# A gated-state attention block between two feed-forwards: each head's state update as a 64-column matmul of its own, and a state read that alternates the heads

## The chip, the cores and the metric
One core of a Trainium2 chip runs the whole program in one launch. The metric is the device time in microseconds; the median of several runs is compared. TensorE's clock has two levels, 1.2 and 2.4 GHz; the profile gives the granted clock as a share of the full one.

## The reference
The input x has 2 sequences of 1024 tokens, 512 wide. The program computes x + 0.5 FFN(norm(x)), then adds attention of the normed result, then adds 0.5 FFN(norm(x)) again. The feed-forward is a two-expert layer with top-1 routing. The change is in the attention alone. It has 16 heads, keys of 64, values of 128 and 64 memory slots per head. With s the clipped slot logits, z their running logsumexp, p = exp(s - z) and g = exp(z[t-1] - z[t]), it is two scans over time:

```python
def step_k(hk, x):
    q_t, k_t, p_t, g_t = x
    hk = hk * g_t[:, :, None, :] + k_t[..., None] * p_t[:, :, None, :]
    return (hk, jnp.einsum('bhk,bhkm->bhm', q_t, hk))
pvT = jax.nn.softmax(okT, axis=-1)
def step_v(hv, x):
    pv_t, v_t, p_t, g_t = x
    hv = hv * g_t[..., None] + p_t[..., None] * v_t[:, :, None, :]
    return (hv, jnp.einsum('bhm,bhmv->bhv', pv_t, hv))
```

The result of the second scan is normed per head, multiplied by a gate and projected by Wo. hk (64 x 64 per head) is called the key state below, hv (64 x 128 per head) the value state.

## The kernel before
The attention works on pairs of heads: eight pairs, the first seven in a hardware loop on every engine, the last written out once more. Within a pair there are four units k = 0 to 3 of 512 tokens, two per sequence, and in a unit four chunks cc of 128 tokens. The scans are done chunk by chunk without the running maximum: with e = exp(s), the state before a chunk is the sum over the earlier chunks of e^T k (key state) or e^T v (value state), and within a chunk a masked score matrix gives the rest. z is the running sum of e, and its reciprocal rz scales the result. A unit with k even starts a sequence ("first" in the code): its chunk 0 has no state to read, so 3 chunks read one, and it forms 4 updates, the last for the next unit. A unit with k odd reads a state in 4 chunks and forms 3 updates.

On 128 partitions the tiles hold both heads of the pair: head h in the partitions 64h to 64h + 63 for what is laid out by feature (qT, kT, eT, pT), and in the columns 64h to 64h + 63 for what is laid out by token (en, kn, the transposed e and k). PSUM is used as six banks R[0] to R[5] of 128 x 512 fp32 and two banks PJ for projections. Plain fp32 tiles go through TensorE as fp32; the projections are split by hand into high and low fp32r parts, three matmuls per product.

The order of TensorE's work in a unit is written out by hand, with the projections of the next unit put between the steps of this one: transposes of z (L1208), project_q of the next unit (L1128), the key state update (L1219, into R[5], signals dk_mm), the scores k^T q of each chunk and head (L1225, heads alternating, 64 partitions each), project_k, the read of the first scan (L1237 with hk, L1239 with the masked scores am; signals ok_mm), project_s and project_vg 0 (L1128, L1154), transposes of the scaled ok (L1250), project_vg 1, the scores of the second scan (L1258, heads alternating, 64 partitions each), the value state update (L1266, signals dv_mm), the masked scores times v (L1273, R[0] and R[1] by head, waits for b_masked), the read of the value state (L1278, waits for hv_done, signals o_mm after each head), project_vg 2 and 3 (L1154), transposes of u (L1294, waits for u_done), transposes of e and k for the next unit (L1191, L1195), and the output projection (L1307).

L1219 multiplies all 128 columns of kn by all of en for a chunk, so the result also has the two products of one head with the other, which nothing reads. L1266 multiplies all 128 columns of en by both heads' 256 columns of v; its four chunks fill two banks, R[2] and R[3], with a signal per bank, and hv is 256 wide, of which each head uses its own half.

VectorE adds the updates up: hk in L1019 and L1021 (64 x 64 pieces, one per head), hv in L1065 and L1067 (one 128 x 256 piece per chunk), each waiting for the one before. Before hv it masks the second scan's scores (L1056), after it come gate_make (L940) and the running sum z_scan (L932). Then follows the chain to the output: ScalarE squares R[0] and R[1] (L887) as the two o_mm signals arrive, VectorE sums (L1085) and adds (L1088), GpSimd raises to the power -0.5 (L772), VectorE multiplies into u (L1092), and TensorE transposes u (L1294).

Before the first pair a ring of six buffers of 512 columns, taken from am, u and hv, receives the rows gathered by DMA from the first feed-forward. In the last pair VectorE, ScalarE and GpSimd also do the norm and routing for the second feed-forward, and there is no next unit after the last one.

Of the kernel before, what the change touches and what calls it, by code (L numbers as in the profile page):

```python
# [28 lines left out]
P = 128  # L29
# [24 lines left out]
UC = UNIT // CHUNK  # L54
# [574 lines left out]
def phase_attention(nc, top, c, watt, gnorm, slot_rows, gather_row, half_weight, xres, norms, routing, loaded, sorted_rows, aw):  # L629
# [9 lines left out]
    with ExitStack() as ctx:  # L639
# [18 lines left out]
        hv = sb("at_hv", [P, UC, 2 * DV])  # L658
# [15 lines left out]
        ring = [x[:, n * D // width:(n + 1) * D // width, :].rearrange("p a b -> p (a b)") for x, width in  # L674
                ((am[:, :, :, :].rearrange("p a b c -> p (a b) c"), P), (u[:, :, :, :].rearrange("p a b c -> p (a b) c"), DV), (hv, 2 * DV)) for n in range(2)]
# [229 lines left out]
        def _(dve):  # L905
# [99 lines left out]
            def pair(i, last_pair):  # L1005
                for k in range(UNITS):
# [47 lines left out]
                    for b in range(2):  # L1054
                        dve.wait_ge(b_mm, count(i, k, 2, b))
                        dve.tensor_tensor(am[:, b, :, :],  # L1056
                                          R[4 + b][:, :].rearrange("p (a t) -> p a t", a=4),
                                          c["causal"][:, :].rearrange("p (a t) -> p a t", a=1).to_broadcast([P, 4, P]), ALU.mult).then_inc(b_masked, 1)
                    for cc in range(UC if first else UC - 1):
                        to = (cc + 1) % UC  # L1060
                        if cc % 2 == 0:
                            dve.wait_ge(dv_mm, count(i, k, 2, cc // 2))
                        part = R[2 + cc // 2][:, (cc % 2) * 2 * DV:(cc % 2 + 1) * 2 * DV]
# [54 lines left out]
        def _(pe):  # L1118
# [80 lines left out]
            def pair(i, last_pair):  # L1199
                for k in range(UNITS):  # L1200
# [17 lines left out]
                    for cc in range(UC if first else UC - 1):  # L1218
                        last = pe.matmul(R[5][:, chunk(cc)], kn[:, cc, :], en[:, cc, :], start=True, stop=True)  # L1219
# [43 lines left out]
                    for b in range(2):  # L1263
                        for a in range(2 if first or b == 0 else 1):
                            cc = 2 * b + a
                            last = pe.matmul(R[2 + b][:, a * 2 * DV:(a + 1) * 2 * DV], en[:, cc, :], v[:, b2, cc, :], start=True, stop=True)  # L1266
                        last.then_inc(dv_mm, 1)
# [8 lines left out]
                    for h in range(2):  # L1276
                        for cc in range(1 if first else 0, UC):
                            last = pe.matmul(R[h][:, chunk(cc)], pT[half(h), chunk(cc)], hv[half(h), cc, h * DV:(h + 1) * DV],  # L1278
                                             start=False, stop=True, skip_group_check=True)
                        last.then_inc(o_mm, 1)  # L1280
# [102 lines left out]
```

## Time and profile before

| | |
|---|---|
| runs, median (lowest to highest) | 2237.46 us (2235.6 to 2238.39), 3 runs |
| profiled execution, span from first to last instruction | 2232.7 us |
| median run beside that span | 4.8 us more |
| TensorE busy with matmuls | 2074.2 us, 93% of the span |
| VectorE busy | 1417.0 us, 63% |
| ScalarE busy | 688.9 us, 31% |
| GpSimd busy | 282.5 us, 13% |
| granted TensorE clock, mean | 0.979 |

The profiled execution's time is known as its span; what lies around it is taken from the difference to the median. A row of the trace gives an engine's instruction or a run of equal ones: start, duration, engine, line, operation, output and inputs, shape, count, and where the engine was idle before it, for how long and what released it. Matmuls are pipelined, so the duration of one is longer than its share of the stream: the distance between the starts of two stages tells what the first one costs. "PE ... 64*128" is a matmul on 64 rows and 128 columns of the array.

### The profile page before, as it was taken

What the parts mean: (1) busy time and instruction counts of PE and PEld (TensorE: products, weight loads), DVE (VectorE), ACT (ScalarE), POOL (GpSimd) and SP (SyncE); (2) the same over time, 40 slices, a digit from 0 to 9 for tenths busy, and PEclk for the clock granted to TensorE, in tenths of its full rate; (3) what the DMA queues carried; (4) which work ended last, traced back from release to release, by engine and by line L of the source; (5) the groups of instructions that cost most, each with busy time, mean ns of one, the idle gap of its engine ahead of it and who ended that gap; (6) DMA issues with size and microseconds to landing.
All of it is one profiled execution on the core that took longest, in us unless ns stands there. A gap on an engine that the chain in (4) does not pass through costs nothing. (4 is left out here: it accounts for less than half of the span.)

```text
span 2232.7 us, 29878 instructions
## 1 busy us (share of the span) xinstructions
PE 2074.2 (93%) x11280; PEld 1739.2 (78%) x11280; DVE 1417.0 (63%) x2579; ACT 688.9 (31%) x1188; POOL 282.5 (13%) x243
## 2 busy tenths in 40 slices
PE   0999999969999999999999999999999569999996
PEld 0888888858888888888888888878888458888885
DVE  6665666766666665665666666665668655665666
ACT  2443444533121221212222221222223134443443
POOL 4000001031020110110110110200202230000004
PEclk9999999979999999999999999999999779999998
DMA  5332333430010000000100100100100062433336
GB/s 205 134 132 94 132 119 130 154 102 8 1 36 9 8 29 8 17 27 1 33 11 1 36 8 1 36 8 1 36 1 20 38 161 95 133 130 101 119 119 245
DMA packets 46926, 149.50 MB, mean 67 GB/s; under 512 B 5856, under 2 KB 5856, under 8 KB 46816
## 3 DMA queue, kind: packets, MB, share of 16 engines
q1 hardware_dynamic: 38544, 121.13, 16.8%
q0 software_dynamic: 8272, 26.76, 3.6%
q8 instruction: 87, 1.43, 0.3%
q14 instruction: 23, 0.19, 0.0%
HBM read 125.83 MB, written 22.04 MB: 66 GB/s over the span
## 5 line engine op out<-in xcount | busy, mean ns | idle before, releaser
L1154 PE MATMUL at_pj<-at_w_lo,at_xT_hi 128*128 128x512 f32 x512 | 207.1, 405 | 0.0
L1154 PE MATMUL at_pj<-at_w_hi,at_xT_hi 128*128 128x512 f32 x512 | 201.0, 392 | 0.0
L1154 PE MATMUL at_pj<-at_w_hi,at_xT_lo 128*128 128x512 f32 x512 | 200.6, 392 | 0.0
L1128 PE MATMUL at_pj<-at_xT_hi,at_w_lo 128*128 128x512 f32 x384 | 162.0, 422 | 0.8 <-DVE at_xT_lo L969 0.8
L503 DVE TENSOR_TENSOR first_ff_w_lo<-first_ff_stage,first_ff_w_hi 128x1024 fp32r<-128x1024 f32 x80 | 98.0, 1225 | 101.1 <-ACT first_ff_w_hi L365 101.1
L503 DVE TENSOR_TENSOR last_ff_w_lo<-last_ff_stage,last_ff_w_hi 128x1024 fp32r<-128x1024 f32 x80 | 97.9, 1224 | 99.4 <-ACT last_ff_w_hi L365 99.4
L1128 PE MATMUL at_pj<-at_xT_lo,at_w_hi 128*128 128x512 f32 x384 | 153.0, 398 | 0.0
L1128 PE MATMUL at_pj<-at_xT_hi,at_w_hi 128*128 128x512 f32 x384 | 152.8, 398 | 0.0
L772 POOL TENSOR_TENSOR at_coef<-at_ms,minus_half 128x4 f32<-128x4 f32 x64 | 63.6, 1010 | 590.9 <-DVE at_ms L1088 590.9
L748 POOL TENSOR_TENSOR at_w_lo<-at_stage,at_w_hi 128x1024 fp32r<-128x1024 f32 (+1 forms) x36 | 78.4, 2178 | 416.7 <-ACT at_w_hi L812 416.7
L1108 DVE TENSOR_TENSOR xres<-at_r,xres 128x512 f32<-128x512 f32 x128 | 88.1, 688 | 61.2 <-PE at_r L1307 61.2
L365 ACT ACTIVATE last_ff_w_hi<-last_ff_stage 128x1024 fp32r<-128x1024 f32 x80 | 84.8, 1060 | 128.2 <-PE last_ff_ps_y L609 117.9
L365 ACT ACTIVATE first_ff_w_hi<-first_ff_stage 128x1024 fp32r<-128x1024 f32 x80 | 84.8, 1060 | 126.4 <-PE first_ff_ps_y L609 118.0
L597 PE MATMUL last_ff_ps_h<-last_ff_xT_hi,last_ff_w_lo 128*128 128x512 f32 (+1 forms) x320 | 119.1, 372 | 3.4 <-DVE last_ff_w_lo L503 2.4
L597 PE MATMUL first_ff_ps_h<-first_ff_xT_hi,first_ff_w_lo 128*128 128x512 f32 (+1 forms) x320 | 118.2, 369 | 1.5 <-DVE first_ff_factor L535 1.3
L597 PE MATMUL first_ff_ps_h<-first_ff_xT_lo,first_ff_w_hi 128*128 128x512 f32 (+1 forms) x320 | 117.8, 368 | 0.0
L597 PE MATMUL last_ff_ps_h<-last_ff_xT_hi,last_ff_w_hi 128*128 128x512 f32 (+1 forms) x320 | 117.7, 368 | 0.0
L597 PE MATMUL first_ff_ps_h<-first_ff_xT_hi,first_ff_w_hi 128*128 128x512 f32 (+1 forms) x320 | 117.7, 368 | 0.0
L597 PE MATMUL last_ff_ps_h<-last_ff_xT_lo,last_ff_w_hi 128*128 128x512 f32 (+1 forms) x320 | 117.7, 368 | 0.0
L1010 DVE RECIPROCAL at_rz<-at_r 128x512 f32<-128x512 f32 x32 | 107.2, 3349 | 11.3 <-PE at_r L1208 11.3
L1154 PEld LDWEIGHTS at_pj<-at_w_lo,at_xT_hi 128*128 128x128 f32 x512 | 96.2, 188 | 22.7
L609 PE MATMUL last_ff_ps_y<-last_ff_w_hi,last_ff_a_lo 128*128 128x512 f32 x288 | 113.1, 393 | 0.8 <-DVE last_ff_a_lo L547 0.8
(283 smaller groups left out, 4921.8 us busy)
## 6 DMA issues: line engine op xcount, KB each, us to landing
first_ff_stage<-wff SPq DMA_DIRECT2D x80, 512.0 KB, 3.2
last_ff_stage<-wff SPq DMA_DIRECT2D x80, 512.0 KB, 3.3
at_stage<-watt SPq DMA_DIRECT2D x24, 512.0 KB, 3.7
at_stage<-watt SPq DMA_DIRECT2D x16, 384.0 KB, 3.3
xres<-x SPq DMA_DIRECT2D x4, 1024.0 KB, 10.2
first_ff_xg<-sorted_rows SPq DMA_DIRECT2D x4, 1024.0 KB, 6.4
slot_rows<-first_ff_y POOLq DMA_DIRECT2D x4, 1024.0 KB, 5.4
last_ff_xg<-sorted_rows SPq DMA_DIRECT2D x4, 1024.0 KB, 7.3
```

What stands on the lines that cost most here:

```text
L365: act.activation(w_hi[:, t % RING, :], stage[:, t % RING, :], ACT.Copy).then_inc(w_hi_done, 1)
L503: dve.tensor_tensor(w_lo[:, t % RING, :], stage[:, t % RING, :], w_hi[:, t % RING, :].bitcast(F32), ALU.subtract).then_inc(w_lo_done, 1)
L597: last = pe.matmul(ps_h[t % 2][:, 0:width], w[:, r, k * P:(k + 1) * P], x[:, k, 0:width], start=(k == 0 and n == 0), stop=(k == KC - 1 and ...
L609: last = pe.matmul(ps_y[i][:, :], x[:, r, i * P:(i + 1) * P], w[:, r, D:2 * D], start=(t == 0 and n == 0), stop=(t == HT - 1 and n == 2))
L748: pool.tensor_tensor(w_lo[:, col:col + width], stage[:, 0:width], w_hi[:, col:col + width].bitcast(F32), ALU.subtract).then_inc(piece_lo, 1)
L772: pool.tensor_tensor(coef[:, cols], ms[:, cols], c["minus_half"][:, cols], ALU.pow).then_inc(coef_done, 1)
L1010: dve.reciprocal(rz[:, :, :], R[2][:, :].rearrange("p (a b) -> p a b", a=UC)).then_inc(rz_done, 1)
L1108: dve.tensor_tensor(xres[:, k * UC + cc, :], R[4 + cc % 2][:, :], xres[:, k * UC + cc, :], ALU.add).then_inc(added, 1)
L1128: last = pe.matmul(PJ[(7 * k + part) % 2][:, :], wq(w, kk, part), x[:, kk, tok], start=(kk == 0 and n == 0), stop=(kk == KC - 1 and n == 2))
L1154: last = pe.matmul(PJ[(7 * k + 3 + t) % 2][:, :], x[:, kk, tok], wvg(w, kk), start=(kk == 0 and n == 0), stop=(kk == KC - 1 and n == 2))
```

## The change
For each chunk the key state update becomes two matmuls, one per head: 64 columns of kn as the stationary operand, 64 columns of en moving, and the result in the head's own half of the partitions. The value state update becomes two matmuls as well: 64 columns of en stationary, the head's 128 columns of v moving, the result in its half of the partitions of R[2], one bank for all four chunks and a single signal dv_mm. hv is 128 wide, and VectorE's additions with it. The read of the value state loops over chunks outside and heads inside, so o_mm is signalled by the last two matmuls. The gather ring takes rz in place of the second half of hv.

```diff
--- before.py
+++ after.py
@@ -655,7 +655,7 @@
         rz = sb("at_rz", [P, UC, P])
         am = sb("at_am", [P, 2, UC, P])
         hk = sb("at_hk", [P, UC, P])
-        hv = sb("at_hv", [P, UC, 2 * DV])
+        hv = sb("at_hv", [P, UC, DV])
         ok = sb("at_ok", [P, UC, P])
         pv = sb("at_pv", [P, UC, P])
         pT = sb("at_pT", [P, UNIT])
@@ -671,8 +671,8 @@
         R = [ctx.enter_context(nc.psum_tensor(f"at_r{b}", [P, 512], F32)) for b in range(6)]
 
 
-        ring = [x[:, n * D // width:(n + 1) * D // width, :].rearrange("p a b -> p (a b)") for x, width in
-                ((am[:, :, :, :].rearrange("p a b c -> p (a b) c"), P), (u[:, :, :, :].rearrange("p a b c -> p (a b) c"), DV), (hv, 2 * DV)) for n in range(2)]
+        ring = [x[:, n, :, :].rearrange("p a b -> p (a b)") for x in (am, u) for n in range(2)]
+        ring += [x[:, :, :].rearrange("p a b -> p (a b)") for x in (hv, rz)]
         xn = [x[:, :, :].rearrange("p a b -> p (a b)") for x in (en, kn, ok, pv)]
         row_added, shift_done, xn_done, x_turned = sem("at_row_added"), sem("at_shift_done"), sem("at_xn_done"), sem("at_x_turned")
         x_hi, x_lo = sem("at_x_hi"), sem("at_x_lo")
@@ -1056,11 +1056,10 @@
                         dve.tensor_tensor(am[:, b, :, :],
                                           R[4 + b][:, :].rearrange("p (a t) -> p a t", a=4),
                                           c["causal"][:, :].rearrange("p (a t) -> p a t", a=1).to_broadcast([P, 4, P]), ALU.mult).then_inc(b_masked, 1)
+                    dve.wait_ge(dv_mm, count(i, k, 1, 0))
                     for cc in range(UC if first else UC - 1):
                         to = (cc + 1) % UC
-                        if cc % 2 == 0:
-                            dve.wait_ge(dv_mm, count(i, k, 2, cc // 2))
-                        part = R[2 + cc // 2][:, (cc % 2) * 2 * DV:(cc % 2 + 1) * 2 * DV]
+                        part = R[2][:, cc * DV:(cc + 1) * DV]
                         if first and cc == 0:
                             last = dve.tensor_copy(hv[:, to, :], part)
                         else:
@@ -1216,7 +1215,9 @@
                     pe.wait_ge(kn_out, count(i, k, 1, 1))
                     pe.wait_ge(added, count(i, k, UC, 0))
                     for cc in range(UC if first else UC - 1):
-                        last = pe.matmul(R[5][:, chunk(cc)], kn[:, cc, :], en[:, cc, :], start=True, stop=True)
+                        for h in range(2):
+                            last = pe.matmul(R[5][half(h), cc * P + 64 * h:cc * P + 64 * h + 64], kn[:, cc, half(h)], en[:, cc, half(h)],
+                                             start=True, stop=True)
                     last.then_inc(dk_mm, 1)
 
                     pe.wait_ge(q_out, count(i, k, 1, 1))
@@ -1260,11 +1261,11 @@
                                 last.then_inc(b_mm, 1)
 
                     pe.wait_ge(v_out, count(i, k, UC, UC))
-                    for b in range(2):
-                        for a in range(2 if first or b == 0 else 1):
-                            cc = 2 * b + a
-                            last = pe.matmul(R[2 + b][:, a * 2 * DV:(a + 1) * 2 * DV], en[:, cc, :], v[:, b2, cc, :], start=True, stop=True)
-                        last.then_inc(dv_mm, 1)
+                    for cc in range(UC if first else UC - 1):
+                        for h in range(2):
+                            last = pe.matmul(R[2][half(h), chunk(cc)], en[:, cc, half(h)], v[:, b2, cc, h * DV:(h + 1) * DV],
+                                             start=True, stop=True)
+                    last.then_inc(dv_mm, 1)
 
 
                     for h in range(2):
@@ -1273,11 +1274,12 @@
                             last = pe.matmul(R[h][:, chunk(cc)], am[:, h, cc, :], v[:, b2, cc, h * DV:(h + 1) * DV],
                                              start=(cc == 0), stop=(first and cc == 0), skip_group_check=True)
                     pe.wait_ge(hv_done, i * HK_AT[UNITS] + HK_AT[k + 1] + 1)
-                    for h in range(2):
-                        for cc in range(1 if first else 0, UC):
-                            last = pe.matmul(R[h][:, chunk(cc)], pT[half(h), chunk(cc)], hv[half(h), cc, h * DV:(h + 1) * DV],
+                    for cc in range(1 if first else 0, UC):
+                        for h in range(2):
+                            last = pe.matmul(R[h][:, chunk(cc)], pT[half(h), chunk(cc)], hv[half(h), cc, :],
                                              start=False, stop=True, skip_group_check=True)
-                        last.then_inc(o_mm, 1)
+                            if cc == UC - 1:
+                                last.then_inc(o_mm, 1)
                     if more:
                         project_vg(i, k + 1, 2)
                         project_vg(i, k + 1, 3)
```

## Rows read from the trace of the kernel before

**Rows 1.** Loop: start:end, length, busy PE, PEld, DVE, ACT, POOL, clock, DMA
```profile
540.00:1690.00 1150.00, 1133.86 (x6769) 954.60 (x6769) 728.92 (x1435) 258.06 (x541) 150.76 (x105) 1.00 0.05 15
```

**Rows 2.** TensorE's waits (total us, times, longest): in the loop, in the whole program
```profile
PE at_r L1208 <- issue: 11.6, 6, 2.2
...
PE at_r L1294 <- DVE at_u L1092: 5.8, 5, 3.8
```

**Rows 3.** TensorE in order of time, a unit with k even (start, duration, then what)
```profile
693.19 0.40 PE L1154 MATMUL at_pj<-at_w_hi,at_xT_hi 128*128 128x512 f32 x1
693.51 1.16 PE L1258 MATMUL at_r<-at_pT,at_eT 64*128 64x128 f32 x16
694.61 1.99 PE L1266 MATMUL at_r<-at_v,at_en 128*128 128x256 f32 x8
696.44 1.95 PE L1273 MATMUL at_r<-at_v,at_am 128*128 128x128 f32 x16
698.31 1.26 PE L1278 MATMUL at_r<-at_hv,at_pT 64*128 64x128 f32 x12
699.51 0.50 PE L1154 MATMUL at_pj<-at_w_lo,at_xT_hi 128*128 128x512 f32 x1
...
705.12 1.04 PE L1294 MATMUL at_r<-ident,at_u 128*128 128x128 f32 x8
706.00 0.60 PE L1191 MATMUL at_r<-ident,at_eT 128*128 128x128 f32 x4
```

**Rows 4.** The same view, a unit with k odd
```profile
810.88 1.56 PE L1266 MATMUL at_r<-at_v,at_en 128*128 128x256 f32 x6
812.28 1.95 PE L1273 MATMUL at_r<-at_v,at_am 128*128 128x128 f32 x16
814.16 1.71 PE L1278 MATMUL at_r<-at_hv,at_pT 64*128 64x128 f32 x16
815.79 0.50 PE L1154 MATMUL at_pj<-at_w_lo,at_xT_hi 128*128 128x512 f32 x1
...
821.40 1.03 PE L1294 MATMUL at_r<-ident,at_u 128*128 128x128 f32 x8
```

**Rows 5.** The same view, the key state with k odd and with k even
```profile
716.03 0.83 PE L1219 MATMUL at_r<-at_en,at_kn 128*128 128x128 f32 x6
716.79 1.16 PE L1225 MATMUL at_r<-at_qT,at_kT 64*128 64x128 f32 x16
...
754.77 1.05 PE L1219 MATMUL at_r<-at_en,at_kn 128*128 128x128 f32 x8
755.76 1.16 PE L1225 MATMUL at_r<-at_qT,at_kT 64*128 64x128 f32 x16
```

**Rows 6.** The same view, matmuls that stream 64 columns, and what follows
```profile
682.85 0.56 PE L1239 MATMUL at_r<-at_en,at_am 128*128 128x64 f32 x4
683.25 0.44 PE L1237 MATMUL at_r<-at_hk,at_qT 128*128 128x128 f32 x2
```

**Rows 7.** The same view, the last unit, where the granted clock is low
```profile
1752.61 2.08 PE L1258 MATMUL at_r<-at_pT,at_eT 64*128 64x128 f32 x16 [0.69 <-ACT at_pT L871]
1754.61 2.75 PE L1266 MATMUL at_r<-at_v,at_en 128*128 128x256 f32 x6
```

**Rows 8.** VectorE in order of time, the unit of rows 3; last row: that of rows 4
```profile
694.71 1.29 DVE L1056 TENSOR_TENSOR at_am<-at_r,causal 128x512 f32<-128x512 f32 x2 [3.10 <-PE at_r L1258]
...
696.36 1.34 DVE L1067 TENSOR_TENSOR at_hv<-at_r,at_hv 128x256 f32<-128x256 f32 x3
...
702.97 2.16 DVE L1092 SCALAR_TENSOR_TENSOR at_u<-at_r,at_coef,at_gate 128x128 f32<-128x128 f32 x8 [1.28 <-POOL at_coef L772]
...
819.03 2.16 DVE L1092 SCALAR_TENSOR_TENSOR at_u<-at_r,at_coef,at_gate 128x128 f32<-128x128 f32 x8 [1.28 <-POOL at_coef L772]
```

**Rows 9.** ScalarE in order of time, the squares of the unit of rows 4
```profile
815.35 1.15 ACT L887 ACTIVATE at_u<-at_r 128x512 f32<-128x512 f32 x2 [4.79 <-PE at_r L1278]
```

**Rows 10.** Weight loads of L1278: duration least/median/most, starts of first and last
```profile
L1278 PEld LDWEIGHTS at_r<-at_hv,at_pT x448: 182/188/188, 541.3 to 1760.4; 64*128 64x128 f32 x150
```

## Prediction

> **What bounds the kernel now.** I read the busy time by stretch first, then TensorE's waits, then its order of time through two units, then VectorE's and ScalarE's. In the attention loop TensorE is busy 1133.86 of 1150 us at full granted clock, and nothing else comes near: VectorE has 728.92 [rows 1]. Over that loop TensorE waits longest at the head of a pass, 11.6 us in six rows with no releaser; for the scaled outputs u (L1294) it waits 5.8 us in the whole program, all of it in the last pair [rows 2]. So a microsecond taken out of TensorE's stream comes off the time one for one, until some result it needs is no longer there when it asks.
>
> Durations of overlapping matmuls mislead; I price a stage by the distance from its start to the start of the next. A "record" below is one MATMUL row: each fp32 matmul of the code leaves two. A unit with k even (u0, 4 chunks of state) and one with k odd (u1, 3 chunks) differ. In u0 the score stage L1258 takes 1.10 us for 16 records, the value state L1266 1.83 for 8, L1273 1.87 for 16, the state read L1278 1.20 for 12 [rows 3]. In u1 the value state takes 1.40 for 6, L1278 1.63 for 16 [rows 4]. The key state L1219 takes 0.99 for 8 and 0.76 for 6 [rows 5].
>
> **The state read (L1278), reordered.** The same records; only heads alternate instead of one head's chunks following the other's. Now a record costs 1.63/16 = 0.102 us; its neighbour L1258 has the same shape (64 rows, 128 columns, N = 128), alternates heads, and costs 1.10/16 = 0.069: two heads stand in different halves of the rows and run side by side. At 0.069, u0 takes 0.82 (saves 0.38) and u1 1.10 (saves 0.54): mean 0.46. Bounds: nothing saved, or 0.49 as a pair at the pace of one single record.
>
> **The value state (L1266).** 8 or 6 records of N = 256 become 16 or 12 of N = 128 with 64 weight columns, each head in its own half of the output partitions. The trace has no matmul on half of the columns. The nearest row is again L1258: also two heads side by side, in halves of the rows. At 0.069 the stage takes 1.10 and 0.82 instead of 1.83 and 1.40: saves 0.73 and 0.58, mean 0.66. If the halves run one after another, the price is L1273's 1.87/16 = 0.117 [rows 3]: 1.87 and 1.40, nothing saved.
>
> **The key state (L1219).** 8 or 6 records of N = 128 become 16 or 12 of N = 64. Below: L1239 (N = 64, full 128 weight columns) costs 0.40/4 = 0.10 a record [rows 6]; streaming 64 columns can't be what costs that, as N = 128 streams within 0.117, so it is the weight load, and half the columns would be half of that, 0.049. Above: 0.069 from L1258. It isn't certain that 0.069 is no issue limit, but at the low clock of the last unit the same 16 records took 2.00 us instead of 1.10 [rows 7], so the array sets it. I take the middle, 0.059: 0.94 and 0.71 instead of 0.99 and 0.76, saves 0.05. The upper bound of cost, serial at 0.10, makes 1.60 and 1.20: 0.52 lost.
>
> **Entries.** Two more changes of the array's shape per unit. Into L1258 the step is 0.32 us instead of 0.23 [rows 3], so up to 0.09 each; into L1225 I find next to nothing. Bounds 0 to 0.18 per unit, I take 0.09. The Trainium skill (TensorEngine Tiling (Array Packing), Key Properties) says that a change of tiling mode drains TensorE, with no price; no row here separates such a drain.
>
> **VectorE and buffers.** The state additions L1067 shrink from 256 to 128 columns: 1.34 us for three with their waits [rows 8] against 0.27 for one of 128 columns (L1092, 2.16/8, rows 8), so the chain ends some 0.5 us earlier. It now waits for the whole stage, not for its half, but it is behind the masks L1056 on VectorE's queue, and those end 1.29 us after 694.71, at 696.00; the value state will be there at 695.7 + 0.2. Four additions of 0.30 end at 697.2; TensorE gets to L1278 at 698.31 - 0.73 = 697.58. Covered by 0.4 us. L1273 wants the second mask at about 696.6; it is there at 696.0. The hk additions read the same halves as before, behind the reciprocal L1010 on VectorE's queue. The gather ring takes rz instead of the second half of hv; it is used only before the first pair: nothing.
>
> **What is late next.** The reads of both heads now end together. In u1 the squares of head 0 began at 815.35, 1.2 us after the stage's start [rows 4, 9]; with both heads in 1.10 us it comes as late, so squares, sums, coefficients and u start earlier by the value state's saving alone, and the read's saving goes to TensorE only. u is finished at 702.97 + 2.16 = 705.13, and its second half is asked for half of L1294's stage of 0.88 after 705.12, at 705.56, in u0 [rows 3, 8]: slack 0.4. In u1: 819.03 + 2.16 = 821.19 against 821.40 + 0.44 = 821.84, slack 0.6 [rows 4, 8]. The read's saving of 0.38 and 0.54 uses both up almost exactly. I allow 0.05 us of new waiting at L1294 in u0.
>
> **Sum.** u0: -0.38 -0.73 -0.05 +0.09 +0.05 = -1.02. u1: -0.54 -0.58 -0.05 +0.09 = -1.08. Seven pairs of two each: -29.4. In the last pair the first unit is a full one (-1.0), in the next two TensorE already waits at L1294, so I count half (-1.1), and the last at low clock waits too: about -1.0. Together -32.5. The profiled execution spans 2232.7 us, the median run is 2237.46: 4.8 us lie around the span and stay. Forecast 2237.5 - 32.5 = 2205.
>
> **Rivals.**
> *Read saving given back.* If the u chain is late by more than my slack, or the read doesn't alternate as L1258 does, 0.46 x 30 = 14 us return as a wait before L1294. For it: slack 0.4 and 0.6 against gains 0.38 and 0.54. Against: the chain's own shift is worked out from rows. Time 2205 + 14 = 2219. Chance 0.12.
>
> *Column halves do not overlap.* Value state 0, key state between 0.049 and 0.10 a record, middle 0.074: +0.19 and +0.12; reads -0.46, entries +0.09: -0.22 a unit, x 31 = -7, time 2230 (from -20 to +4 by the key state's price). For it: no row shows this shape, and both halves need all 128 rows at once, with two different moving streams. Against: nothing in the trace. Chance 0.18.
>
> *The weight load is exposed: slower.* Place: between the records of L1219 and L1266. Load 0.049 plus streaming 0.107 (N = 128, within the 0.102 of L1278 and the 0.117 of L1273) or 0.053 (N = 64, half of it): value state 2.50 and 1.87 (+0.67, +0.47), key state 1.63 and 1.22 (+0.64, +0.46), mean +1.12; with -0.46 and +0.09 +0.75 a unit, x 31 = +23, time 2260. It decides from a price per record: both stages take 2.49 us a unit now and will have 28 records, so with 0.37 of credit it is slower from (2.49 + 0.37)/28 = 0.102 us on their mean. Against it: L1278's records of one head load weights for 188 ns each into the same rows [rows 10] yet follow one another within 0.102, so loads do go on beside matmuls in the same rows. The Trainium skill (TensorE: Matmul & The Clock Gate, Part 3, The mechanism) states that a weight load overlaps with matmuls in flight only where the row group differs. By that rule both heads' halves, which use all rows, would be this rival; L1278's rows speak against its strict form. Chance 0.10.
>
> The forecast itself keeps 0.60.
>
> **The numbers.** Under the forecast, key state at 0.049 and no entry cost save 0.2 more a unit, and pairs at the pace of a single record (0.107) 0.25 more: 2191; the poor ends (0.069, entries at 0.18, 0.1 more of waiting) cost 0.33 a unit: 2215. The first two rivals reach 2219 and 2230. Range 2190 to 2231: out are the exposed load and the worse half of the second rival. A measurement of this kernel tells about 0.2%, 4.5 us, from no change. Faster: 0.60 + 0.12 + 0.13 of the second rival = 0.85. Same 0.05, slower 0.10.
>
> **What the changed profile would show.** L1278 to the next L1154: 0.8 and 1.1 us. The value state with 16 and 12 records in 1.1 and 0.8 us; if 1.9 and 1.4, the halves don't overlap; if 2.5, the load is exposed. The key state near 0.9 and 0.7. L1092's release of the u transposes appears among TensorE's waits for a few tenths at most. In the loop a unit should be 1.05 us shorter than before, VectorE's hv additions 0.27 us each, and the feed-forward stages the same. I am wrong if the state stages grow, or if TensorE idles before the u transposes by half a microsecond in every unit.

## The result, and the profile after

The changed kernel takes 2201.32 us in the median of four runs (2197.42 to 2204.29), the kernel before 2237.67 beside it; the ratio is 0.984, 95% interval 0.9826 to 0.9854. That is 36.4 us less, against a forecast of 32.5. The profiled execution of the changed kernel took 2204.29 us with a span of 2202.6, so 1.7 us lie around the span; in the profiled execution of every later kernel it is 1.6 to 1.8 us. The prediction had set 4.8 us there for the kernel before, from the median of several executions, so its profiled execution was probably a quicker one than the median. The forecast took a difference from the median, so the 4.8 us do not enter it.

The changed kernel's page, busy time by engine, and below it the loop of pairs by stretch, with the columns of [rows 1]:

```profile
PE 2041.8 (93%) x11728; PEld 1698.0 (77%) x11728; DVE 1400.3 (64%) x2579; ACT 687.8 (31%) x1188; POOL 281.7 (13%) x243
```

```profile
540.00:1655.00 1115.00, 1097.87 (x7159) 910.76 (x7158) 711.98 (x1432) 255.83 (x539) 149.84 (x104) 1.00 0.05 16
```

More records, less time: 11728 matmul rows instead of 11280, and TensorE's share of the loop is where it was, 98%. The loop is still bound by it, so what was taken out of it came off. TensorE in order of time, one unit with k even (compare [rows 3]), then its key state and the two stages of a unit with k odd (compare [rows 4, 5]):

```profile
688.67 1.16 PE L1259 MATMUL at_r<-at_pT,at_eT 64*128 64x128 f32 x16
689.76 1.09 PE L1266 MATMUL at_r<-at_v,at_en 128*64 128x128 f32 x16
690.78 2.05 PE L1274 MATMUL at_r<-at_v,at_am 128*128 128x128 f32 x16
692.77 0.94 PE L1279 MATMUL at_r<-at_hv,at_pT 64*128 64x128 f32 x12
693.63 0.50 PE L1153 MATMUL at_pj<-at_w_lo,at_xT_hi 128*128 128x512 f32 x1
...
699.25 1.04 PE L1296 MATMUL at_r<-ident,at_u 128*128 128x128 f32 x8
700.13 0.60 PE L1190 MATMUL at_r<-ident,at_eT 128*128 128x128 f32 x4
700.57 0.60 PE L1194 MATMUL at_r<-ident,at_kT 128*128 128x128 f32 x4
701.36 0.47 PE L1309 MATMUL at_r<-at_w_hi,at_uT_lo 128*128 128x512 f32 x1 [0.19 <-DVE at_uT_lo L1100]
...
709.91 0.39 PE L1127 MATMUL at_pj<-at_xT_hi,at_w_hi 128*128 128x512 f32 x1
710.23 0.57 PE L1219 MATMUL at_r<-at_en,at_kn 128*64 128x64 f32 x12
710.73 1.16 PE L1226 MATMUL at_r<-at_qT,at_kT 64*128 64x128 f32 x16
...
727.35 0.88 PE L1266 MATMUL at_r<-at_v,at_en 128*64 128x128 f32 x12
728.20 2.05 PE L1274 MATMUL at_r<-at_v,at_am 128*128 128x128 f32 x16
730.18 1.16 PE L1279 MATMUL at_r<-at_hv,at_pT 64*128 64x128 f32 x16
731.27 0.50 PE L1153 MATMUL at_pj<-at_w_lo,at_xT_hi 128*128 128x512 f32 x1
...
747.80 0.69 PE L1219 MATMUL at_r<-at_en,at_kn 128*64 128x64 f32 x16
748.42 1.16 PE L1226 MATMUL at_r<-at_qT,at_kT 64*128 64x128 f32 x16
```

From start to start, before and after:

| stage | k even | k odd |
|---|---|---|
| value state | 1.83 to 1.02 | 1.40 to 0.85 |
| masked scores times v, behind it | 1.87 to 1.99 | 1.88 to 1.98 |
| read of the value state | 1.20 to 0.86 | 1.63 to 1.09 |
| key state | 0.99 to 0.62 | 0.76 to 0.50 |
| last projection matmul ahead of the key state | 0.23 to 0.32 | 0.23 to 0.32 |
| sum of the changes | -1.31 | -1.16 |

From the transposes of z of one unit to those of the next, the loop units (median of seven passes) went from 38.87, 38.76 and 38.73 us (k = 0, 1, 2) to 37.55, 37.59 and 37.44: 1.32, 1.17 and 1.29 less. The table accounts for it; no wait for u appeared in the loop.

The last pair did not follow. Its two middle units went from 40.00 and 40.39 us to 41.08 and 41.18. TensorE's busy time there by 3 us, columns as in [rows 1], in the changed kernel:

```profile
1653.00:1656.00 3.00, 2.20 (x14) 1.97 (x15) 2.90 (x13) 1.81 (x5) 0.84 (x1) 0.86 0.00 0
1656.00:1659.00 3.00, 3.00 (x11) 2.47 (x10) 1.52 (x3) 0.42 (x1) 2.16 (x3) 0.57 0.46 175
```

TensorE had waited for u, and behind the wait the granted clock fell to its lower level, 1.2 GHz, for some 3 us. More on that below.

### The profile page after: what moved, and what is told of

Read it like the earlier page. It is cut to its first block and busy times, and to the rows that moved or that the text cites. A ratio compares the mean times of both kernels' runs of the same rounds, so it can differ in the third digit from the quotient of the medians.

```text
span 2202.6 us, 30742 instructions
## 1 busy us (share of the span) xinstructions
PE 2041.8 (93%) x11728; PEld 1698.0 (77%) x11728; DVE 1400.3 (64%) x2579; ACT 687.8 (31%) x1188; POOL 281.7 (13%) x243
```

## The experiments

Each time is compared with that of the kernel before, run beside it on the same chip.

Some of the readings below need more than the time of a whole stage. In the trace every matmul record has its own start, which the view in order of time puts together for a run of equal ones; where the text says "record by record", the distances between these single starts are meant. The values given are medians over the 28 loop units or stand so in every loop unit looked at.

**The three parts alone.** In the kernel before, only the loops of the read were turned, and the signal o_mm goes with them:

```diff
-                    for h in range(2):
-                        for cc in range(1 if first else 0, UC):
+                    for cc in range(1 if first else 0, UC):
+                        for h in range(2):
...
-                        last.then_inc(o_mm, 1)
+                            if cc == UC - 1:
+                                last.then_inc(o_mm, 1)
```

> Only the read of the value state alternates the heads; both state updates stay as before. Theory (two heads in different row halves run side by side, 0.069 us a record): the stage L1278 falls from 1.20 to 0.83 us (k even) and from 1.63 to 1.09 (k odd), no wait for u appears in the loop, and the time falls by 0.36 and 0.54 a unit, 31 units: 14 us less, 2224. Rival (the read's saving is given back as a wait for u, since both results now come at the end): the stages shrink the same, but waits before the transposes of u of 0.3 to 0.5 us a unit stand in the trace and the time stays at 2234 to 2238.

Measured: 2226.59 us against 2236.62, ratio 0.996 (0.9946 to 0.9974), 10.0 us less. The stage takes 0.86 and 1.09 us, loop units are 0.34 and 0.56 us shorter, and no wait for u stands in the loop: the theory's mechanism. The full 14 us are not there: the loop alone gives 28 x 0.45 = 12.6, and medians scatter by two or three. In the last pair TensorE now waits 1.03 and 1.13 us for u where it waited 0.48 and 0.81, and the two units take 40.05 and 40.39 us, as before. There the rival holds: the read's saving is given back whole.

The key state alone:

```diff
-                        last = pe.matmul(R[5][:, chunk(cc)], kn[:, cc, :], en[:, cc, :], start=True, stop=True)
+                        for h in range(2):
+                            last = pe.matmul(R[5][half(h), cc * P + 64 * h:cc * P + 64 * h + 64], kn[:, cc, half(h)], en[:, cc, half(h)],
+                                             start=True, stop=True)
```

> Only the key state update is split by head. Theory (column halves run side by side and the weight load of 64 columns is half as long): the stage takes 0.62 us with 16 records and 0.50 with 12, as in the changed kernel, and its entry costs 0.09: 0.28 and 0.17 less a unit, 31 units: 7 us less, 2231. Rival (the gain needs the other two edits, or the halves run in turn): stage of 0.9 us or more, time at 2236 to 2242.

Measured: 2227.29 us against 2236.62, 0.996 (0.9946 to 0.9974), 9.3 us less, with stages of 0.61 and 0.50 us. In the loop it is 0.29 us a unit with k even and 0.20 with k odd; the theory holds, within what runs scatter.

The value state alone, which is the changed kernel with key state and read put back:

```diff
-                        for h in range(2):
-                            last = pe.matmul(R[5][half(h), ...
+                        last = pe.matmul(R[5][:, chunk(cc)], kn[:, cc, :], en[:, cc, :], start=True, stop=True)
...
-                    for cc in range(1 if first else 0, UC):
-                        for h in range(2):
+                    for h in range(2):
+                        for cc in range(1 if first else 0, UC):
...
```

> Only the value state update is split by head, with hv 128 wide and one signal; the read keeps one head after the other, the key state is as before. Theory (halves side by side): stage 1.02 us with 16 records and 0.85 with 12, the stage behind it 0.11 longer, 0.70 and 0.44 less a unit, 31 units: 18 us less, 2220. The three parts done alone then add up to 39 us against the 36 measured for all together, the rest being what the last pair gives back. Rival (the shorter additions on VectorE are what helps): the stage stays near 1.8 us.

Measured: 2220.15 us against 2236.62, 0.9922 (0.9908 to 0.9935), 16.5 us less; stages of 1.03 and 0.85 us and 1.98 behind them, units 0.69 to 0.74 (k even) and 0.46 us (k odd) shorter. TensorE's stage itself shrank, so it is not VectorE's shorter additions that helped. The parts add up: 10.0 + 9.3 + 16.5 = 35.8 us against 36.4. That is within the scatter of the medians, and the units say the same more sharply: with k = 2, 0.32 + 0.29 + 0.69 = 1.30 us against 1.29. So none of them needs another.

**Do the column halves run side by side?** The changed kernel with the head loop outside in both state updates:

```diff
-                    for cc in range(UC if first else UC - 1):
-                        for h in range(2):
+                    for h in range(2):
+                        for cc in range(UC if first else UC - 1):
```

> The changed kernel, but both state updates take all chunks of head 0 and then all of head 1, so that neighbouring records use the same half of the columns. Same records, same shapes. Theory (the gain is two column halves running side by side): value state back to 16 x 0.107 to 0.117 = 1.7 to 1.9 us and 1.3 to 1.4, key state 16 x 0.05 to 0.10 = 0.8 to 1.6 us; at least 0.6 us a unit lost against the changed kernel: 2201 + 19 or more = 2220 to 2245. Rival (the smaller weights are what helps, whatever the order): stages stay at 1.02 and 0.62 us, time 2201.

Measured: 2217.22 us against 2236.62, 0.9909 (0.9896 to 0.9923). TensorE in order of time, the value state of a unit with k even, a unit with k odd and the key state of the next:

```profile
692.67 1.58 PE L1266 MATMUL at_r<-at_v,at_en 128*64 128x128 f32 x16
694.18 2.05 PE L1274 MATMUL at_r<-at_v,at_am 128*128 128x128 f32 x16
...
713.65 0.73 PE L1219 MATMUL at_r<-at_en,at_kn 128*64 128x64 f32 x12
714.31 1.16 PE L1226 MATMUL at_r<-at_qT,at_kT 64*128 64x128 f32 x16
...
730.93 1.15 PE L1266 MATMUL at_r<-at_v,at_en 128*64 128x128 f32 x12
732.01 2.05 PE L1274 MATMUL at_r<-at_v,at_am 128*128 128x128 f32 x16
...
751.61 0.97 PE L1219 MATMUL at_r<-at_en,at_kn 128*64 128x64 f32 x16
752.50 1.16 PE L1226 MATMUL at_r<-at_qT,at_kT 64*128 64x128 f32 x16
```

The value state takes 1.08 us with 12 records and 1.51 with 16, the key state 0.66 and 0.89. The four records between them cost 0.43 us, 0.1075 each, and 0.23, 0.057 each. Record by record, two of the same half start 0.109 us apart for N = 128 and 0.058 for N = 64. The order of the same records is worth 0.77 us in a unit with k even and 0.39 with k odd, 16 us on the program: running side by side is most of the gain of both updates, and the rival of the smaller weights falls. The time expected, 2220 to 2245 us, was missed by 3 us, and the stages came out 0.2 us shorter than expected.

The single starts say why. The 16 records of a value state with k even start 0.160, 0.109, 0.109, 0.109, 0.006, 0.103, 0.057, 0.053, 0.056, 0.053, 0.056, 0.110, 0.109, 0.109 and 0.109 us apart. Two streams of eight records, each 0.160 and then 0.109 us apart, give these distances within 0.002 us if the second starts with the fifth record of the first. With 12 records the second starts with the third of six. The trace does not name the head of a record, but the reading leaves little else: although the code gives all of head 0 first, four records of each half still ran side by side. So this kernel is not the pure one-after-the-other case, and the order is worth more than it shows here. The state read of the kernel before has the same pattern, which is why a record of it cost 0.102 us and not the 0.112 at which its first ones follow each other.

Even so this kernel beats the one before by 19.4 us, of which the read is 10. The key state is still 0.10 us shorter than with full columns, which its entry takes back, and the value state 0.32, of which 0.11 comes back on the stage behind it. The value state gains there, with as many columns streamed as before, by the records that overlap: 16 of them at 0.109 with nothing side by side would be 1.74 us and more with the ends of the stage, and it takes 1.51.

**The true pace of a pair.** The changed kernel with both state updates issued twice; the second writes the same values over the first:

```diff
-                    for cc in range(UC if first else UC - 1):
+                    for cc in 2 * list(range(UC if first else UC - 1)):
```

> The changed kernel with every matmul of both state updates issued twice (the second overwrites the first with the same values). It gives the price of a record without the ends of a stage: the stage with 32 records less the one with 16. Theory (two halves side by side, each streaming at full pace: 0.0535 us a record of N = 128, 0.027 of N = 64): the value state grows by 0.86 us with k even, the key state by 0.43. Rival (the 0.043 and 0.030 read from 16 less 12 records are the true pace): 0.68 and 0.48.

Measured, in a single run: 2234.61 us. TensorE in order of time:

```profile
755.64 1.15 PE L1219 MATMUL at_r<-at_en,at_kn 128*64 128x64 f32 x32
756.72 1.16 PE L1226 MATMUL at_r<-at_qT,at_kT 64*128 64x128 f32 x16
...
773.13 1.97 PE L1266 MATMUL at_r<-at_v,at_en 128*64 128x128 f32 x32
775.03 2.05 PE L1274 MATMUL at_r<-at_v,at_am 128*128 128x128 f32 x16
```

1.90 us instead of 1.02 and 1.08 instead of 0.62: 0.88 us and 0.46 us for 16 more records, 0.055 and 0.029 each. For the value state that is the theory: two halves of the columns, each at full pace, cost half of the 0.109 of one. For the key state the theory (0.027) and the rival (0.030) lie on either side of 0.029; there the single starts decide. Record by record the two of a pair start 0.007 us apart, and pairs follow each other every 0.109 us (N = 128) and 0.058 us (N = 64), the same distance as two records of one half. The difference between the value state with 16 and with 12 records, 0.043, was no pace: with 12 records the last one is followed at 0.245 us, with 16 at 0.203.

The same reading of L1259 and L1279, two heads in halves of the rows, gives pairs every 0.112 us, and L1274, which fills the array, has a record every 0.112. So halves of the rows run side by side at full pace too, 0.056 us a record. The 0.069 of the prediction is that pace with the ends of a stage of 16 records spread over it: its first pair takes 0.213 us and its last 0.21. A stage of small matmuls is priced by doubling it or record by record, not by dividing a short one.

**How much slack is left for u.** The changed kernel with one more sum over 512 columns ahead of head 0's:

```diff
+                        if b == 0:
+                            dve.tensor_reduce(ss[:, 4:8], u[:, b, :, :], op=ALU.add, axis=AX.X)
                         dve.tensor_reduce(ss[:, cols], u[:, b, :, :], op=ALU.add, axis=AX.X).then_inc(ss_done, 1)
```

> The changed kernel with one more sum over 512 columns on VectorE (0.6 to 0.7 us) ahead of head 0's sum, so that u is ready that much later. It measures how much slack the changed kernel has left before the transposes of u. Theory (0.1 us left in a unit with k even, somewhat more with k odd): waits for u of 0.3 to 0.6 us in every unit of the loop, time up by 28 x 0.45 = 13 us or more, 2214, and more if the clock falls behind a wait. Rival (slack of half a microsecond or more is left): no waits in the loop, time up by 2 us at most.

Measured: 2211.91 us, 11.1 more than the changed kernel on the same chip (2200.81). TensorE in order of time:

```profile
738.96 0.60 PE L1298 MATMUL at_r<-ident,at_u 128*128 128x128 f32 x4
739.92 0.66 PE L1298 MATMUL at_r<-ident,at_u 128*128 128x128 f32 x4 [0.35 <-DVE at_u L1093]
740.41 0.60 PE L1192 MATMUL at_r<-ident,at_eT 128*128 128x128 f32 x4
740.85 0.60 PE L1196 MATMUL at_r<-ident,at_kT 128*128 128x128 f32 x4
741.20 0.49 PE L1311 MATMUL at_r<-at_w_hi,at_uT_lo 128*128 128x512 f32 x1
```

A chain 0.6 us later lengthens the stage of the u transposes from 0.88 to 1.46 us: hardly 0.1 us of slack was left for the second half of u, as the prediction had it. The waits of the theory are there, 0.35 to 0.37 us in the loop, but its price for them is not. The first half comes without a wait, so it has more slack, and the unit grows by only 0.17 to 0.24 us, some 6 us over 28 units (the last pair's two middle units grow too, to 41.68 and 41.54), for something else shrinks: from the transposes of k to the output projection it is 0.35 us here, and 0.79 in the changed kernel (700.57 to 701.36), with 0.19 of idle time waiting for the low part of u's first half. The kernel before has the same gap, 0.80 us in the unit of [rows 3]. It suggests an edit.

**A version that beats both.** The transposes of u's first half go ahead of the last three matmuls of the projection before them, in the loop pairs only. Its high and low parts are then made while those three matmuls run:

```diff
-            def project_vg(i, k, t):
+            def project_vg(i, k, t, inside=None):
...
                 for kk in range(KC):
+                    if inside is not None and kk == KC - 1:
+                        inside()
...
-                        project_vg(i, k + 1, 3)
+                        project_vg(i, k + 1, 3, inside=None if last_pair else lambda: turn_u(i, k, 0))
...
-                    for b in range(2):
...
+                    for b in range(0 if last_pair else 1, 2):
+                        turn_u(i, k, b)
```

turn_u(i, k, b) holds the wait, the four transposes and the signal that stood in the loop over b.

> The changed kernel with the transposes of the first half of u put ahead of the last three matmuls of the projection before them, in the loop pairs only. Theory (TensorE stands idle some 0.34 us a unit ahead of the output projection, for the low part of u's first half; that half has 0.7 us of slack, the second only 0.1): the idle time goes, two more steps between fp32 and fp32r cost 0.09 each, 0.1 to 0.25 us a unit less, 28 units: 3 to 7 us less than the changed kernel, 2196. Rival (the first half of u isn't ready 0.7 us earlier): a wait ahead of the transposes takes the place of the idle time, time 2200 to 2205.

Measured: 2192.71 us (2191.53 to 2194.92), ratio to the kernel before 0.9807 (0.9793 to 0.982); the changed kernel on the same chip 2199.07 (2195.65 to 2202.53), 0.9829 (0.9816 to 0.9843). 6.4 us less, and no run of one lies among those of the other.

```profile
698.40 0.66 PE L1204 MATMUL at_r<-ident,at_u 128*128 128x128 f32 x4
698.81 0.48 PE L1155 MATMUL at_pj<-at_w_lo,at_xT_hi 128*128 128x512 f32 x1
...
699.60 0.60 PE L1204 MATMUL at_r<-ident,at_u 128*128 128x128 f32 x4
700.04 0.60 PE L1192 MATMUL at_r<-ident,at_eT 128*128 128x128 f32 x4
700.48 0.60 PE L1196 MATMUL at_r<-ident,at_kT 128*128 128x128 f32 x4
700.83 0.48 PE L1314 MATMUL at_r<-at_w_hi,at_uT_lo 128*128 128x512 f32 x1
```

The output projection follows the transposes of k at 0.35 us, no wait is left in the loop but that at the head of a pass, and loop units take 37.24, 37.32 and 37.19 us, 0.25 to 0.3 less.

The same in the last pair too:

> The same in the last pair too, where u comes later than TensorE asks for it. Theory: there the earlier transposes wait up to 0.7 us longer with the three matmuls behind them, nothing is gained or lost beyond 1 us against the kernel with it in the loop alone: 2196 to 2198. Rival (the longer single wait makes the clock fall more often): 2 to 4 us more.

Measured: 2194.56 us, 0.9819 (0.9804 to 0.9834), 1.9 above the one before with intervals that overlap: no gain there, and no loss that this can tell. In the last pair u comes late and TensorE waits 2.12 and 2.34 us ahead of the three matmuls.

**The last pair and the clock.** The changed kernel, but in the last pair the read takes one head after the other:

```diff
+                    order = [(cc, h) for cc in range(1 if first else 0, UC) for h in range(2)]
+                    if last_pair:
+                        order.sort(key=lambda x: x[1])
...
```

> The changed kernel, but in the last pair the read takes all chunks of head 0, then all of head 1, as before. Theory (in the last pair the saved time comes back as a longer wait for u, 1.06 and 1.31 us instead of 0.48 and 0.81, behind which the granted clock falls to about half for 3 us and costs 1.6 us, twice): TensorE's own work grows by 0.5 us a unit, the waits shrink by about as much, the clock stays at 1.00 behind them, units 2 and 3 of the last pair take 39.5 instead of 41.1 us, and the time is 2 to 4 us less than the changed kernel's: 2198. Rival (the longer units come of VectorE's routing work alone, whatever TensorE does): units stay at 41 us, time 2201.

and the changed kernel twice again:

> The changed kernel itself, on the same chip as the three runs before, to compare with. Both theories: 2197 to 2205, with the spread coming of stretches at half clock behind idle time: the fewer in a run, the nearer to 2197.

> The changed kernel on the same chip, to compare the two before with: 2198 to 2203.

Measured: 2204.2 us (2200.06 to 2205.48) beside 2200.81 (2198.59 to 2212.68) for the changed kernel on the same chip; and 2199.07 (2195.65 to 2202.53) in the third set. In the profiled run the waits for u shrank to 0.52 and 0.97 us, the two middle units took 39.46 and 39.59 and the clock stayed up, as expected; but the program gained nothing that the runs could show. The third set suggests why. There the changed kernel itself waited the same 1.08 us, and the clock behind it stayed at 1.00. TensorE's row, then the stretches:

```profile
1653.59 0.66 PE L1296 MATMUL at_r<-ident,at_u 128*128 128x128 f32 x4 [1.08 <-DVE at_u L1091]
```

```profile
1653.00:1656.00 3.00, 2.04 (x17) 1.80 (x18) 2.90 (x13) 1.72 (x5) 0.68 (x1) 1.00 0.00 0
1656.00:1659.00 3.00, 3.00 (x16) 2.45 (x15) 2.33 (x6) 0.41 (x1) 2.33 (x3) 1.00 0.46 175
```

Its middle units took 39.45 and 39.62 us. So whether the clock falls behind a wait of this length differs from run to run: twice in the first profile of the changed kernel, once in the second (39.44 and 41.12 us), never in the third. Each fall costs 1.6 us. The same happens behind the longest waits of the loop, at the head of a pass. The second of two in the first profile:

```profile
1432.61 0.65 PE L1207 MATMUL at_r<-ident,at_zT 128*128 128x128 f32 x4 [2.32 <-issue]
```

A first unit of 39.1 us instead of 37.55 stands twice in the first and third profile and in none of the second. The kernel before has such a unit as well, 40.38 us instead of 38.87, behind a wait of 1.89 us, and none behind its waits of 2.19 and 2.23: the length of the wait alone does not decide. With four falls, one and two, the spans are 2202.6, 2196.8 and 2200.8 us. The second and the first differ by 5.8 us, of which three falls are 4.8. The second and the third differ by 4.0, of which one fall is only 1.6, so falls in the attention are a part of the scatter and not all of it. In other executions of the second set the granted clock goes with the time: a span of 2198.3 us at a mean of 0.979, one of 2210.9 at 0.973. The 0.006 are 13 us of 2200, worked out from these two, against the 12.6 between the spans. No run held the clock up on purpose.

**Where a change of shape costs.** The key state update goes behind the scores:

```diff
-                    for cc in range(UC if first else UC - 1):
-                        for h in range(2):
-                            last = pe.matmul(R[5][half(h), ...
-                    last.then_inc(dk_mm, 1)
...
                                 last.then_inc(a_mm, 1)
+                    for cc in range(UC if first else UC - 1):
+                        for h in range(2):
+                            last = pe.matmul(R[5][half(h), ...
+                    last.then_inc(dk_mm, 1)
```

> The changed kernel with the key state update behind the scores of the first scan instead of ahead of them; hk is ready 1.1 us later. It tells what a change of the array's shape costs by its place. Theory (an entry from the fp32r projections into a smaller shape costs 0.09 us whichever shape it is, and from 64-row to 64-column records nothing more): TensorE's part is unchanged, VectorE is ready with the masks 0.2 us before they are needed or just late, time 2201 to 2205. Rival (each change of shape drains the array and costs 0.1 us by itself): the distance from the last scores to the key state and from the key state to the projections each grows by 0.1.

Measured: 2216.76 us, 0.9894 (0.9879 to 0.9909), 16 us more than the changed kernel beside it. A unit with k even, TensorE and then VectorE:

```profile
751.27 1.16 PE L1221 MATMUL at_r<-at_qT,at_kT 64*128 64x128 f32 x16
752.36 0.69 PE L1226 MATMUL at_r<-at_en,at_kn 128*64 128x64 f32 x16
756.41 0.66 PE L1240 MATMUL at_r<-at_en,at_am 128*128 128x64 f32 x4 [0.37 <-DVE at_am L1026]
```

```profile
753.10 0.46 DVE L1019 COPY at_hk<-at_r 64x64 f32<-64x64 f32 x2 [1.00 <-PE at_r L1226]
753.59 1.44 DVE L1021 TENSOR_TENSOR at_hk<-at_r,at_hk 64x64 f32<-64x64 f32 x6
755.06 1.29 DVE L1026 TENSOR_TENSOR at_am<-at_r,causal 128x512 f32<-128x512 f32 x2
```

On TensorE the scores take 1.09 us and the key state 0.62, as in the other order. That does not make the step between them free, and it does not settle the rival of a drain at each change of shape. Either order has three changes: from the projections into the first stage, between the two, and out of the second. A cost for each would leave the sum as it is, and so it is. Nothing in this experiment could tell the two expectations apart.

The single starts can. Where the shape stays, a record or a pair of N = 128 is followed at 0.105 to 0.112 us. Where it changes, the last record before the change is followed at 0.20 us: full array to 64 rows 0.205, 64 rows to full array 0.202, 64 rows to 64 columns 0.202, 64 columns to full array 0.203. From the key state to the scores, with N = 64 on 64 columns, it is 0.152 instead of 0.051. Behind the change the second record, or pair, comes 0.10 us later than usual, into 64 columns 0.05. So every change costs, the one between 64 rows and 64 columns like the others, and the kernel before had most of them already. New in the changed kernel are two per unit: into the key state, and out of the value state into the full array.

The time went elsewhere: VectorE stands idle for 1.00 us until hk's first piece is there, and the masks behind the additions on its queue end at 756.35. TensorE's step onto L1240 is 0.77 us instead of 0.23, with 0.37 of it put down as a wait for the mask, and the record behind comes 0.10 later, so a unit is longer by 0.6 to 0.7 (k even) and 0.13 (k odd). My margin of 0.2 us for VectorE was wrong in the even units: they have eight pieces of hk, and I had taken a unit with six. Neither expectation had the time right.

## Why the prediction was right

The direction, the mechanism and the order of the terms were right, and 2201.32 lies 4 us under 2205. By its steps:

- **TensorE bounds the loop, one for one.** Right: the stage differences of -1.31 and -1.16 us are the differences of the units, 34.6 us over the 28 loop units, where the terms of the forecast gave 29.4.
- **The state read at L1258's pace.** Right to 0.04 us: 0.86 and 1.09 us where 0.82 and 1.10 stood. The first run of one part shows it alone.
- **The value state as a pair of heads in column halves.** Right in kind, 0.08 short with k even (1.02 instead of 1.10) and 0.03 over with k odd (0.85 instead of 0.82). The halves of the rows were a good measure: both kinds of half run at full pace, pairs every 0.112 and 0.109 us. The 0.069 a record was right as a price for a stage of this length, with its ends in it, and not as a pace; what differs is mostly the first pair, 0.160 instead of 0.213 us.
- **The key state.** The term that was mis-sized: 0.94 and 0.71 forecast, 0.62 and 0.50 measured. The prediction took 0.049 for the weight load of 64 columns as the least that a record can cost, half of L1239's 0.10, and the middle of that and 0.069. The half was about right: record by record L1239 takes 0.111 (its first distance alone is 0.058), and records of one column half 0.058 (this is also half of the 0.109 of N = 128, so the rows do not tell whether load or stream sets it). What the prediction missed is that the other half's record costs nothing beside it: 0.029 a record, under its lower bound. It is worth 0.32 and 0.21 us a unit beyond the forecast.
- **Entries.** Forecast 0.09 a unit; measured 0.09 ahead of the key state and 0.11 on the stage behind the value state, 0.20, just over the upper bound of 0.18. Reading "next to nothing" for the step into L1225 was wrong: the key state's last record is followed there at 0.205 us instead of 0.112, which the stage of the key state contains. The Trainium skill (TensorEngine Tiling (Array Packing), Key Properties) has TensorE drained at a change of mode. The single starts agree: at every change of shape looked at they show 0.09 to 0.10 us ahead of it and 0.05 to 0.10 behind.
- **VectorE's chain behind the value state.** Right: additions of 0.28 us and no wait of the read for hv.
- **What is late next.** Right in the loop: no wait for u, with 0.1 us left, which the run with the later chain confirms. The 0.05 allowed in u0 was not needed.
- **The last pair.** Right without the clock: -0.55 and -0.77 us in the third profile against a forecast of -0.55 each. Wrong in leaving out that behind such a wait the clock can fall: with it the units grew by 1.08 and 0.79. In the profiled execution the two falls took back some 3 us of the 5 that the loop gave beyond the forecast, so its 2204.29 lies nearer to 2205 than the terms do; that part of the agreement is luck.

The rival of the exposed weight load is refuted, even its premise. With the halves in turn, records of one column half and of all 128 rows follow each other at 0.109 us for 128 streamed columns and 0.058 for 64, where the rival had 0.156 and 0.102. A load left in the open would add to that. The rule of the Trainium skill (TensorE: Matmul & The Clock Gate, Part 3, The mechanism), that a weight load overlaps only with matmuls of another row group, doesn't hold in that form here. The rival of column halves that don't overlap is refuted by the same run. The rival of a saving given back is false in the loop and true in the last pair, for the read alone.

## What to carry to other kernels

Where a product of two heads wastes half of its result, give each head its own half of the array's columns and let consecutive matmuls alternate: the same records cost 0.055 us alternating and 0.109 one behind the other in the same half, so the order of the loops decides, not the smaller shape. A trace row of the same trick in the other dimension (halves of the rows) priced the value state within 0.1 us; the key state, with shorter matmuls, it priced 0.3 too dear. Count the changes of shape that the trick adds, and read a pace from single records, for the ends of a stage of 16 are 0.15 to 0.20 us of its 0.6 to 1.1. After such a gain look at what was just in time before: here each half of u has its own slack, and spending the first half's bought another 6.4 us.

## What the runs showed of the hardware

- Two fp32 matmuls on the two column halves of the array run side by side at full pace: pairs of records start every 0.109 us for N = 128 and every 0.058 for N = 64, as far apart as two records of one half. Doubling the stages gives the same, 0.055 and 0.029 us a record.
- Two on the row halves with 128 weight columns do so too: pairs every 0.112 us at N = 128, where records that fill the array start every 0.112.
- With 64 streamed columns a record with 128 weight columns costs 0.111 us (L1239), one with 64 weight columns 0.058.
- At a change between full array, 64 rows and 64 columns the last record before it is followed 0.09 to 0.10 us later than otherwise, and the first behind it 0.05 (into 64 columns) to 0.10 us later. It holds between 64 rows and 64 columns as well.
- When one half's records all come ahead of the other's, the last four of the first half and the first four of the second still overlap, with 12 records and with 16, as the single starts are read above.
- Behind a wait of TensorE of 1.1 to 1.3 us, with another 0.4 soon after, or of 1.9 to 2.3 at the head of a pass, the granted clock falls in some runs and not in others, for about 3 us and 1.6 us of time.
